# Attention scores on Trainium2: the second pass of long score rows as two 64-row products side by side

## The reference, cut to what matters

```python
x = x + 0.5 * ffn(layernorm(x), ...)            # x is (8, 1024, 256)
x = x + attention(layernorm(x), Wq, Wk, Wv, Wo, span_val)
x = x + 0.5 * ffn(layernorm(x), ...)

def attention(query, Wq, Wk, Wv, Wo, span_val): # 16 heads of 64
    q, k, v = heads(query @ Wq), heads(query @ Wk), heads(query @ Wv)
    w = einsum('bhqd,bhkd->bhqk', q, k) / 64 + causal    # the scores
    w = softmax(w)
    w = w * mask                                 # a ramp over the key position, per head
    w = w / (sum(w) + 1e-8)
    return merge(einsum('bhqk,bhkd->bhqd', w, v)) @ Wo
```

## Time and profile before

| what | us |
|---|---|
| median of 3 runs | 3326.25 (3323.58 to 3326.55) |
| profiled execution | 3324.66, span 3322.9, granted TensorE clock 0.987 |
| TensorE busy in that span | 3153.8 |
| VectorE busy | 2712.9 |
| ScalarE busy | 2424.1 |
| first pass of the scores (L1476), 1536 matmuls | 502.1 busy |
| second pass (L1477), 1536 matmuls | 481.8 busy |

### The profile page before, as it was taken

One profiled execution on the slowest core, in us unless ns is written; L12 is line 12 of the kernel. 1 busy time (PEld: TensorE's weight loads), 2 busy tenths in 40 slices (PEclk: granted clock), 3 DMA queues, 4 the chain that ended last, 5 costly groups with the idle time before them and its releaser, 6 DMA issues.

```text
span 3322.9 us, 77451 instructions
## 1 busy us (share of the span) xinstructions
PE 3153.8 (95%) x28851; PEld 2412.3 (73%) x28851; DVE 2712.9 (82%) x5152; ACT 2424.1 (73%) x4769; POOL 1521.8 (46%) x1743
## 2 busy tenths in 40 slices
PE   4999997999999999999999999999999999799998
PEld 2677775777777777777777777777777777477776
DVE  7999995777877877777787778777777777799997
ACT  4677764777777777777778777777777777566664
POOL 2344332454555455455455455545545544233332
PEclk9999998999999999999999999999999999899999
DMA  3133313223322232222233223223222323111111
GB/s 112 39 91 89 116 39 89 52 58 77 81 58 69 65 90 68 65 77 73 53 84 79 60 65 85 66 59 96 68 52 59 93 59 101 33 52 58 58 58 39
DMA packets 160355, 231.34 MB, mean 70 GB/s; under 512 B 30064, under 2 KB 72176, under 8 KB 159984
## 3 DMA queue, kind: packets, MB, share of 16 engines
q1 hardware_dynamic: 159984, 226.38, 25.1%
HBM read 93.27 MB, written 32.38 MB: 38 GB/s over the span
## 4 chain that ended last, share of the span: by engine, by line
PE 69%; issue 6%; DVE 5%; ACT 2%; POOL 2%; DVEq 0%; ACTq 0%; POOLq 0%
PE at_t_ps L1487 14%; PE at_o_ps L1503 10%; PE at_side_ps L1401 10%; PE ffn_gu_ps L511 7%; PE at_s_ps L1476 6%; PE at_s_ps L1477 6%; PE at_side_ps L1454 4%; PE at_side_ps L1413 4%; PE ffn_down_ps L536 4%; DVE at_e_rows L1669 2%; PE at_side_ps L1442 2%; ACT at_eT_hi L1585 1%; PE ffn_hT_ps L481 1%; DVE at_eT_lo L1675 1%; DVE at_v_masked L1647 1%
## 5 line engine op out<-in xcount | busy, mean ns | idle before, releaser
L1675 DVE SCALAR_TENSOR_TENSOR at_eT_lo<-at_t_ps,at_eT_hi 128x512 f16<-128x512 f32 (+3 forms) x1536 | 853.7, 556 | 470.6 <-ACT at_eT_hi L1585 444.3
L1577 ACT ACTIVATE at_e_rows<-at_e_rows,at_neg_max 128x1024 f32<-128x1024 f32 (+7 forms) x1024 | 792.1, 774 | 215.7 <-DVE at_neg_max L1669 214.2
L1585 ACT ACTIVATE at_eT_hi<-at_t_ps 128x512 f16<-128x512 f32 (+3 forms) x1536 | 745.8, 486 | 189.5 <-PE at_t_ps L1487 180.7
L1669 DVE CUSTOM_DVE_ANT_0 at_e_rows<-at_s_ps,at_strip,keep_s_scale 128x1024 f32<-128x1024 f32 (+7 forms) x1024 | 828.7, 809 | 10.2 <-PE at_s_ps L1477 7.4
L1487 PE MATMUL at_t_ps<-at_ident,at_e_rows 128*128 128x128 f32 x4608 | 801.5, 285 | 0.1
L1503 PE MATMUL at_o_ps<-at_v_cols,at_eT_hi 128*128 128x132 f16 x4608 | 610.7, 221 | 11.0 <-ACT at_o_raw L1596 6.5
L1503 PE MATMUL at_o_ps<-at_v_cols,at_eT_lo 128*128 128x66 f16 x4608 | 568.0, 193 | 0.0
L1476 PE MATMUL at_s_ps<-at_kh_st,at_q_st 128*128 128x512 f16 (+3 forms) x1536 | 502.1, 327 | 18.1 <-DVE at_acc L1659 12.5
L1503 PEld LDWEIGHTS at_o_ps<-at_v_cols,at_eT_hi 128*128 128x128 f16 x4608 | 433.3, 97 | 91.5 <-DVE at_eT_lo L1675 24.0
L1487 PEld LDWEIGHTS at_t_ps<-at_ident,at_e_rows 128*128 128x128 f32 x4608 | 493.3, 141 | 4.1 <-issue 0.5
L1477 PE MATMUL at_s_ps<-at_kl_st,at_q_st 128*128 128x512 f16 (+3 forms) x1536 | 481.8, 327 | 0.0
(11 more groups left out here) (245 smaller groups left out, 6544.9 us busy)
## 6 DMA issues: line engine op xcount, KB each, us to landing
at_kh_st<-at_k_hi SPq DMA_DIRECT2D x256, 128.0 KB, 2.3
at_kl_st<-at_k_lo SPq DMA_DIRECT2D x256, 128.0 KB, 2.3
at_w_qk<-w_qk_split SPq DMA_DIRECT2D x65, 256.0 KB, 3.0
at_q_st<-at_q_hi SPq DMA_DIRECT2D x128, 128.0 KB, 2.4
at_q_st<-at_q_lo SPq DMA_DIRECT2D x128, 128.0 KB, 2.4
at_w_v<-w_v_split SPq DMA_DIRECT2D x66, 128.0 KB, 2.3
ffn_x_rows<-in_L_attn_query_dram SPq DMA_DIRECT2D x32, 256.0 KB, 3.2
ffn_x_res<-in_L_attn_query_dram SPq DMA_DIRECT2D x32, 256.0 KB, 3.8
```

Source lines behind the costliest of these rows:

```text
L1577: nc.scalar.activation(e_rows[:, n % 4, :w], e_rows[:, n % 4, :w], ACT.Exp, bias=neg_max[:, n % 4:n % 4 + 1], scale=-1.0).then_inc(sem("ex ...
L1585: nc.scalar.activation(eT[0][:, i % EBUF, :count * P], t_ps[i % TBUF][:, :count * P], ACT.Copy, scale=PSCALE).then_inc(sem("eT_hi"), 1)
L1669: nc.vector.tensor_tensor_reduce(e_rows[:, n % 4, :w], s_ps[n % 2][:, col:col + w], strip[:, SEQ - w:], keep["s_scale"][:, 0:1], BIGGEST, ...
L1675: nc.vector.scalar_tensor_tensor(out=eT[1][:, i % EBUF, :count * P], in0=t_ps[i % TBUF][:, :count * P], scalar=PSCALE, in1=eT[0][:, i % EB ...
```

## The change

Four edits belong together. `score_chunks` cuts a long row in two halves of w/2 columns instead of at 512; each half still has a PSUM bank of its own. A new set of tiles `q_hh` holds a second copy of q's high part in partitions 64 to 127 (partitions 0 to 63 are not used), which takes two more transfers per pair of heads. In `scores` the first pass runs over both halves as before with all 128 partitions; then the second pass of a long unit is two matmuls over 64 partitions each: the left half of the keys with q's high part in partitions 0 to 63, the right half with the copy in 64 to 127. The small product q_low·k_low, which the stacked second pass gave along, is thus no longer computed for long units. Short units are as before. `row_max` reads the two halves of the scores as a pattern of two pieces, 512 columns apart.

```diff
 def score_chunks(j):
     w = P * (j + 1)
-    return [(0, 0, w)] if w <= CHUNK else [(0, 0, CHUNK), (CHUNK, CHUNK, w - CHUNK)]
+    return [(0, 0, w)] if w <= CHUNK else [(0, 0, w // 2), (CHUNK, w // 2, w // 2)]
...
+        q_hh = [[sb(f"q_hh{i}{a}", [P, SEQ], F16) for a in range(2)] for i in range(2)]
...
-                for n, tiles in (("q", [(q_st, 0, 0), (q_st, 1, 1)]), ("k", [(kh_st, 0, 0), (kh_st, 0, 1), (kl_st, 1, 0), (kl_st, 1, 1)])):
+                for n, tiles in (("q", [(q_st, 0, 0), (q_st, 1, 1), (q_hh, 0, 1)]), ("k", [(kh_st, 0, 0), (kh_st, 0, 1), (kl_st, 1, 0), (kl_st, 1, 1)])):
...
                 chunks = score_chunks(j)
-                for ci, (col, k0, w) in enumerate(chunks):
-                    lastc = ci == len(chunks) - 1
-                    out = s_ps[n % 2][:, col:col + w]
-                    qs = q_st[par][a][:, j * P:(j + 1) * P]
-                    nc.tensor.matmul(out, qs, kh_st[par][a][:, k0:k0 + w], start=True, stop=False)
-                    last = nc.tensor.matmul(out, qs, kl_st[par][a][:, k0:k0 + w], start=False, stop=True)
+                rows = slice(j * P, (j + 1) * P)
+                for col, k0, w in chunks:
+                    nc.tensor.matmul(s_ps[n % 2][:, col:col + w], q_st[par][a][:, rows], kh_st[par][a][:, k0:k0 + w], start=True, stop=False)
+                if len(chunks) == 1:
+                    last = nc.tensor.matmul(s_ps[n % 2][:, 0:w], q_st[par][a][:, rows], kl_st[par][a][:, 0:w], start=False, stop=True)
+                else:
+                    for half, (col, k0, w) in enumerate(chunks):
+                        part = slice(half * DH, (half + 1) * DH)
+                        last = nc.tensor.matmul(s_ps[n % 2][:, col:col + w], (q_st, q_hh)[half][par][a][part, rows], kl_st[par][a][part, k0:k0 + w],
+                                                start=False, stop=True)
...
-                col = score_chunks(j)[0][0]
                 w = P * (j + 1)
+                parts = len(score_chunks(j))
+                split = lambda ap: ap.rearrange("p (h c) -> p h c", h=parts)
+                scores = s_ps[n % 2][:].rearrange("p (h c) -> p h c", c=CHUNK)[:, :parts, :w // parts]
...
-                nc.vector.tensor_tensor_reduce(e_rows[:, n % 4, :w], s_ps[n % 2][:, col:col + w], strip[:, SEQ - w:], keep["s_scale"][:, 0:1], BIGGEST,
+                nc.vector.tensor_tensor_reduce(split(e_rows[:, n % 4, :w]), scores, split(strip[:, SEQ - w:]), keep["s_scale"][:, 0:1], BIGGEST,
```

More of the change, by code:

```diff
@@ L1271, in rest_free @@
                 for par in range(2):
-                    sp.wait_ge(sem(f"q_placed{par}"), 64 * (BATCH * PAIRS // 2))
+                    sp.wait_ge(sem(f"q_placed{par}"), 96 * (BATCH * PAIRS // 2))
                     sp.wait_ge(sem(f"k_placed{par}"), 128 * (BATCH * PAIRS // 2))
@@ L1465, in scores @@
                 if n == 0:
-                    pe.wait_ge(sem(f"q_placed{par}"), g * 32 + (64 if par == 0 else 32))
+                    pe.wait_ge(sem(f"q_placed{par}"), g * 48 + (96 if par == 0 else 48))
                     pe.wait_ge(sem(f"k_placed{par}"), g * 64 + (128 if par == 0 else 64))
```

## The result

The changed kernel takes 3334.69 us (median of 8 runs, 3331.93 to 3335.62) against 3322.90 us of 8 runs of the kernel before on the same chip: a ratio of 1.0034, 95% interval 1.0026 to 1.0043, so 9 to 14 us slower. The forecast was 3294.

What follows compares the result with a forecast made beforehand. TensorE was taken to bound the kernel: -89.5 saved, +15.4 stagger and +33.8 switches give -40 us, times 0.8 = -32, +1 at the start; 3294 us beside 3326.25 (-1.0%). Range 3255 to 3412.

Steps and rivals of the forecast that it cites:

- What bounds the kernel: Attention: TensorE sets the pace, scores hold 12% of the chain (399 us); large added time counts 1.0, filling pauses up.
- a worth of 0.8 a microsecond: Scores on TensorE: each microsecond saved shortens the kernel by about 0.8 us.
- What is removed: Second pass of 512 long units on TensorE: 212,992 columns saved, 89.5 us.
- the stagger: Between the two 64-row products: the right half starts 0.03 us late, 15.4 us in all; bounds 0 and 0.09 us.
- The switch: TensorE from 128 rows to 64 and back, 1024 times: 0.033 us each, 33.8 us in all.
- The break-even: Price per change between 128 and 64 rows on TensorE at which no gain is left: 0.072 us.
- rival 2: Ahead of and behind the 64-row products, each switch empties TensorE: 0.163 us, 167 us in all, 3419; chance 0.32.
- Elsewhere: Off TensorE: two-piece row maximum adds 0, placing transfers fit SP's free 3.1 us, added bytes cost nothing.
- The 1 us put down for the start: At the very start, placing the first pair has nothing beside it: up to 1.2 us show, 1 taken.
- Rival 1: TensorE, 128 and 64 rows in turn: no switch price, -59 us, 3267, or 3254 without stagger; chance 0.18.
- Rival 3: The 64-row halves run one after the other, nothing saved, switches remain: +34 us, 3360; chance 0.05.
- Rival 4: VectorE, or ScalarE's waits for the maxima, take over; a microsecond is worth 0.1: -4 us, 3322; chance 0.09.

Runs made afterwards that it cites:

- the kernel with full rows: Changed kernel, but the second pass of long units contracts over all 128 rows again, other edits kept: 3324.65 us, ratio 1.0007 to the kernel before.
- the kernel with the same rows: Changed kernel, but both 64-row products lie in rows 0 to 63: 3385.59 us, ratio 1.0188 to the kernel before, 51 us slower than the changed kernel.
- the four cases after a pause: Matmuls alone: 128 or 64 rows after 128 or 64, behind a pause where VectorE answers; median 57 ns from VectorE's end to start in all.

## Why the prediction was wrong

**What bounds the kernel: right, but read too far.** TensorE has hardly a pause, and the engines beside it have room. But the step from 12% of the chain to a worth of 0.8 a microsecond failed: with the switches away the saved 89.5 us gave 41, 0.46. The chain tells what lay on it in one execution, not what comes next to it: TensorE's share fell to 60% as soon as it was faster. The reverse claim, that an added microsecond costs 1.0 since it fills the pauses, had its own reason upside down: filling pauses is what makes the first added ones cheap (51 of 88), and 0.85 came only afterwards.

**What is removed: right.** 212,992 columns, and the products do run side by side. The bound 0 was the nearest for the stagger: 3 ns instead of the 30 taken, 1.5 us instead of 15.4. The weight load and the issue between the two products, given as the reason for a stagger, don't keep them apart.

**The switch: this step sank the forecast.** It was taken at 0.033 us from the nearest row, four transposes after FP16 products; it is 0.096 on the way in and 0.103 on the way out. The row shows a late second transpose behind a very short product, not a change of the height in use. With the measured prices the sum reads -89.5 + 1.5 + 512 x 0.199 = +13.9 us on TensorE, 13.6 by the starts, and with the product behind each unit, a term that the prediction didn't have, 19. Of these 11.8 show in all, 10.0 against the kernel with full rows: 0.5 to 0.6, like the first added microseconds of the kernel with the same rows. That 13.9 and 11.8 lie so near each other is chance. The break-even was given as 0.072 us, with the measured stagger it is 0.086; the truth lies above, so rival 2 held in its sign, and in its mechanism so far: the overlap across the border is lost, as the weight loads and the four cases after a pause show. Its price of 0.163 us, a matmul's whole tail, was an upper bound, and 0.6 of that is paid: in the timeline of the changed kernel the second pass starts at 1542.57, and the product before it has its modelled end at about 1542.63. The Trainium skill, "TensorEngine Tiling (Array Packing)", section "Key Properties", has the drain at a change of mode and none at a change of tile within it. The runs agree on where the price is paid: 0.1 us at every border between heights, nothing between the halves. That it is a drain and nothing else they don't show. I weighed that rule below a row that only resembled the case.

**The sum, the range and the chances.** 3324.66 - 32 + 1 + 1.6 is 3295 and not 3294, which changes nothing. The measured 3334.69 lies within 3255 to 3412, but that range was drawn to hold both signs, so this is no success: the forecast was a gain of 1.0%, and slower had a chance of 0.37.

**Elsewhere: right.** The row maximum kept 1276 ns, no wait for placing appeared, and SP had the gap for the transfers. The 1 us put down for the start isn't excluded by the 2 us (-0.7 to 5.3) of the kernel with full rows; where these come from, if they are there, stays open.

**The rivals.** Rival 1's condition didn't come, and its price was too high: with no switch the kernel stands at 3283, not 3267, since the worth was off. Rival 3 was excluded by the 51 us. Rival 4, that something else takes over, isn't what made the change slow, but it is why a perfect version of it would bring 41 us and not 72.

**A version that beats both** wasn't found. An excursion to 64 rows costs 0.21 us, about 500 columns at 0.42 ns. A unit of 1024 saves 512, the others less. If the second pass of a short unit were done in the same excursion as that of a long one, at most 576 columns would be saved each time (half of 4608 columns in four excursions, each 0.24 us): an estimate of 0.03 us for each of 512 excursions, 17 us on TensorE and about 8 at the worth of 0.46, at the edge of what can be measured. It would need scores a unit earlier, and wasn't tried.

## What to carry to other kernels

Products side by side in the two halves of the array double the rate, but each border between tile heights costs about 0.1 us of overlap. Count the columns saved for each excursion against 500 at the full clock, gather the work of one height, or put the border where TensorE waits anyway. Before a saving on the busiest engine is priced, leave the work out once and look: here, with TensorE busy for 98% of the stretch, 0.46 of it showed. Pauses shorter than a matmul's tail don't stand among the waits: look at the starts.

## What was unexpected of the hardware

The granted clock fell while the engine was without a pause. In the kernel of matmuls alone, stretches with 128-row products or with both 64-row halves in use are at 1.00 (2.4 GHz). After 40 products in rows 0-63 alone (8.6 us) and during those that alternate with rows 0-31, it is at half, 1.2 GHz; it returned once full-height products and pairs came again. Whether the height in use or the borders between them matter here, one run can't tell. The stretches (us; PE busy, other engines, granted clock, DMA):

```profile
135.00:150.00 15.00, 15.00 (x177) 7.29 (x177) 0.00 (x0) 0.00 (x0) 1.00 0.00 1
150.00:165.00 15.00, 15.00 (x58) 5.17 (x55) 0.00 (x0) 0.00 (x0) 0.92 0.00 0
165.00:180.00 15.00, 15.00 (x29) 2.80 (x28) 0.00 (x0) 0.00 (x0) 0.50 0.00 1
...
195.00:210.00 15.00, 15.00 (x75) 3.43 (x76) 0.00 (x0) 0.00 (x0) 0.83 0.00 0
210.00:225.00 15.00, 15.00 (x94) 3.69 (x90) 0.00 (x0) 0.00 (x0) 1.00 0.00 1
```

The attention doesn't see this: its clock stayed as before. And a product that follows a switch at one remove still starts about 10 ns late (226 instead of 216), a transpose 56 ns (165 instead of 109); why, no run shows.
